# Graph-attention head 1 gets its own vector buffer, head 2's weights come in two halves: a transfer schedule is rearranged

## The chip, the core and the metric

The kernel is one program on one core of a Trainium2 chip. Its engines are named as in the profile: PE is TensorE (PEld its weight load), DVE VectorE, ACT ScalarE, POOL GpSimd, and SP the sync engine, whose queue issues nearly all large transfers. The metric is the device time of one execution in microseconds. Three executions of the kernel before took 346.65, 346.98 and 348.58 us; the median is 346.98.

## The reference

Four layers follow each other, each with a graph part and a feed-forward part, over 128 nodes with 768 features. The change touches only the first graph layer, a graph attention network (GAT) with eight heads. It comes after a layernorm of x:

```
def gat_layer(x, W, a_s, a_d, b, edge_index, concat):
    h = (x @ W).reshape(n, H, C)
    alpha_s = jnp.einsum('nhc,hc->nh', h, a_s)
    alpha_d = jnp.einsum('nhc,hc->nh', h, a_d)
    e = leaky_relu(alpha_s[src] + alpha_d[dst], 0.2)
    ... softmax over the edges of each dst, then
    msg = h[src] * alpha[:, :, None]
    out = segment_sum(msg, dst)
```

For head h there are 768 x 768 weights of the first product (2304 KB), two attention vectors of 768 (one for sources, one for targets) and 768 x 768 weights of the second layer's product, into which the eight heads are summed. All values are float32. Heads are counted from 0 here, so the "second head" is head 1 and the "third head" is head 2.

## The kernel before, in words

Everything is written out by hand: each engine has its own list of instructions, and semaphores order them against each other. x sits transposed in `xT` as six chunks. The first product of a head, x times its weights, is `head_product` (the matmuls of L1591; for head 0 they stand at L1654). It runs over six chunks of the contraction, first for one part of the output columns (512, six matmuls) and then for the rest (256, six more); a float32 matmul shows as two instructions in the trace. ACT copies the result into `h1`, whose halves alternate by head (`par`), and signals `h_rows`. DVE's `head_alphas` (L855, L857) multiplies those rows with the head's two attention vectors in `avec` and sums. These two numbers per node are turned by PE in `score_row` (L1599), DVE and ACT make the masked softmax (`head_softmax`, L867 to L877), PE turns it (`turn_attention`, L1605), aggregates (`aggregate_head`, L1613), DVE adds the bias (L885, signal `z_ready`) and applies the activation in three steps, and PE runs the second product (`head_second`, L1625).

The heads are pipelined: while PE multiplies head h+1, the attention of head h is computed beside it. PE's instructions are strictly in order. During head 1's first product PE also counts the edges (`count_edges`, 33 small bf16 matmuls at L1661) after three chunks and takes head 0's `score_row` after four; during head 2's first product head 1's `score_row` stands behind three chunks. That `score_row` waits for `alpha_ready` (head 1's numbers), for `score_sum`, and for `z_ready` of head 0, which on DVE stands behind head 1's `head_alphas`.

The transfers go through SP's queue in program order. Weights land in ring slots: the first products alternate between slots 0 and 1, the second products between 2 and 3. `x` comes first, then head 0's weights in six pieces, the first half of head 1's weights (semaphore `w1_second_in`), the vectors of head 0, and the second half of head 1's weights (semaphore `w1_in1`). After that a loop over steps issues, for each step, the next head's first weights (behind `hprod`, the end of the product that used the slot), this head's vectors (behind `alpha_ready`, because there is one buffer `avec`) and the previous head's second weights. A semaphore rises by 16 with each transfer that has landed completely.

Of the kernel before, what the change touches and what calls it, by code (L numbers as in the profile page):

```python
# [18 lines left out]
ALU = mybir.AluOpType  # L19
# [3 lines left out]
P = 128  # L23
D = 768
C = D // P
UNIT = C * D
# [86 lines left out]
def build(nc, a, out):  # L113

    ctx = ExitStack()
    with ctx:
        def sb(name, shape, dt=F32):
            return ctx.enter_context(nc.sbuf_tensor(name, shape, dt))
# [12 lines left out]
        g3 = sb("g3", [P, D])  # L131
        g4 = sb("g4", [P, D])
        h1 = sb("h1", [P, 2 * D])
        h2 = sb("h2", [P, 2 * D])
        avec = sb("avec", [P, 2 * D])
        row0 = sb("row0", [P, D])
        row1 = sb("row1", [P, D])
        rows = sb("rows", [P, NROWS])
        cols = sb("cols", [P, NCOLS])
        shiftm = sb("shiftm", [P, 3 * P])  # L140
# [52 lines left out]
        def slot_part(k, lo=0, hi=UNIT, parts=P):  # L193

            return ring[0:parts, SLOT_AT[k] + lo:SLOT_AT[k] + hi]
# [20 lines left out]
        S = {}  # L216

        def s(name):

            if name not in S:  # L220
                S[name] = sem(name)
            return S[name]
# [95 lines left out]
        def wait(eng, name, value):  # L318

            if value >= 1:  # L320
                eng.wait_ge(s(name), value)
# [3 lines left out]
        def chained(eng, name, ins):  # L325

            used[name] += 1
            ins.then_inc(S[name], 1)
            eng.wait_ge(S[name], used[name])

        def first_chunk(c):

            return f"w1_first{c}_in" if c < C - 1 else "w1_in0"
# [9 lines left out]
        @block.sync  # L343
        def _(sp):
            def load_avec(h):

                wait(sp, "alpha_ready", h)
                sp.dma_start(avec[:], a["gat_a"][bass.ds(h, 1), :].broadcast_to([P, 2 * D])).then_inc(S["avec_in"], 16)

            def load_w1(h, par):  # L350

                if h >= 2:
                    sp.wait_ge(S["hprod"], h - 1)
                sp.dma_start(slot_part(par), a["gat_w1"][bass.ds(h, 1)].rearrange("o p n -> (o p) n")) \
                    .then_inc(S[f"w1_in{par}"], 16)

            def load_w2(h, par):

                if h >= 2:
                    sp.wait_ge(S["w2_used"], h - 1)  # L360
                sp.dma_start(slot_part(2 + par), a["gat_w2"][bass.ds(h, 1)].rearrange("o p n -> (o p) n")) \
                    .then_inc(S[f"w2_in{par}"], 16)

            def load_step(h, par):
                load_w1(h + 1, 1 - par)
                load_avec(h)
                load_w2(h - 1, 1 - par)

            def load_unit(u):
                slot = landed[u][0]  # L370
                for name, c0, parts, n in UNITS[u]:
                    to, of = slot_part(slot, c0, c0 + n, parts), a[name]
                    if name in SHARED:
                        lo, hi = SHARED[name]
                        to = to.rearrange("p (c n) -> p c n", c=C)[:, :, lo:hi]
                        of = of.rearrange("p (c n) -> p c n", c=C)
                    sp.dma_start(to, of).then_inc(S[f"slot{slot}_in"], 16)

            sp.dma_start(x[:], a["x"]).then_inc(S["x_in"], 16)

            w1_0 = a["gat_w1"][0:1].rearrange("o p n -> (o p) n")
            for c in range(C):
                sp.dma_start(slot_part(0, c * D, (c + 1) * D), w1_0[:, c * D:(c + 1) * D]).then_inc(S[first_chunk(c)], 16)
            half = UNIT // 2
            w1_1 = a["gat_w1"][1:2].rearrange("o p n -> (o p) n")
            sp.dma_start(slot_part(1, 0, half), w1_1[:, 0:half]).then_inc(S["w1_second_in"], 16)
            load_avec(0)
            sp.dma_start(slot_part(1, half, UNIT), w1_1[:, half:UNIT]).then_inc(S["w1_in1"], 16)
            for h in range(1, 7):
                load_step(h, h % 2)  # L390
            load_avec(7)
            load_w2(6, 0)
            sp.wait_ge(S["hprod"], 7)
            load_unit(0)
            load_w2(7, 1)
            load_avec(8)

            for u in (U_L1, U_L1W1A, U_L1W1B, U_L2, U_L1W2A, U_L1W2B, *range(U_L3A, len(UNITS))):  # L400
                if u == U_L1:
                    sp.wait_ge(S["hprod"], 8)
                if u == U_L1W1A:
                    sp.wait_ge(S["w2_used"], 7)
                if u == U_L1W1B:
                    sp.wait_ge(S["hprod"], 9)
                if u == U_L2:
                    sp.wait_ge(s("edges_summed"), 1)
                if u >= SLOTS:
                    sp.wait_ge(s(released[u - SLOTS][0]), released[u - SLOTS][1])  # L410
                if u - SLOTS == U_L2:
                    sp.wait_ge(s("w_quantised"), 1)
                load_unit(u)
            for n, (lo, hi) in enumerate(HALVES):
                sp.wait_ge(s("result_ready"), n + 1)
                sp.dma_start(out[:, lo:hi], xb[:, lo:hi]).then_inc(S["out_done"], 16)
            sp.wait_ge(S["out_done"], 32)
# [360 lines left out]
        def _(dve):  # L778
            def link(ins):
                chained(dve, "dve_step", ins)  # L780
# [68 lines left out]
            def head_alphas(h, par):  # L849

                wait(dve, "h_rows", h + 1)
                dve.wait_ge(S["avec_in"], 16 * h + 16)
                wait(dve, "alpha_ready", h)
                hp = h1[:, par * D:(par + 1) * D]
                link(nc.vector.tensor_tensor_reduce(g3[:], hp, avec[:, 0:D], 1.0, 0.0, ALU.mult, ALU.add,  # L855
                                                    alpha[:, par, 0:1]))
                nc.vector.tensor_tensor_reduce(g4[:], hp, avec[:, D:2 * D], 1.0, 0.0, ALU.mult, ALU.add,  # L857
                                               alpha[:, par, 1:2]).then_inc(S["alpha_ready"], 1)

            def head_softmax(h, par):  # L860
# [109 lines left out]

            share = cell("alpha_share", 4)
            dve.wait_ge(s("gat2_rows"), 1)
            dve.wait_ge(S["avec_in"], 16 * 9)
            dve.wait_ge(S["alpha_ready"], 8)
            for k in range(2):
                link(nc.vector.tensor_tensor_reduce(g3[:, 0:WIN], h1[:, 0:WIN], avec[:, k * D:k * D + WIN], 1.0, 0.0, ALU.mult,
# [509 lines left out]
        def _(pe):  # L1486
# [78 lines left out]
            def head_product(n, par, in_value, after_first=None, halfway=None):  # L1565

                if n == 1:
                    pe.wait_ge(S["w1_second_in"], 16)
                else:
                    pe.wait_ge(S[f"w1_in{par}"], in_value)  # L1570
                if n >= 2:
                    pe.wait_ge(S["h_rows"], n - 1)
                w = slot_part(par).rearrange("p (c n) -> p c n", c=C)
                at = 0 if par == 0 else WIN + 256
                parts = ((0, WIN), (WIN, D)) if par == 0 else ((256, D), (0, 256))
                for lo, hi in parts:
                    if lo != parts[0][0]:

                        if after_first is not None:
                            after_first()  # L1580
                        wait(pe, "h_rows", n)
                    for c in range(C):
                        if c == 3 and lo == parts[0][0] and halfway is not None:
                            halfway()
                        if n == 1 and c == 3 and lo == parts[0][0]:
                            pe.wait_ge(S["w1_in1"], in_value)
                        if n == 1 and c == 4 and lo == parts[0][0]:
                            score_row(0, 0)
                        if n == 1 and c == 3 and lo == parts[1][0]:
                            turn_attention(0)  # L1590
                        last = mm(ps[:, at + lo:at + hi], xT[:, c, :], w[:, c, lo:hi], start=(c == 0), stop=(c == C - 1))  # L1591
                return last

            def score_row(h, par):

                wait(pe, "alpha_ready", h + 1)
                wait(pe, "score_sum", h)
                wait(pe, "z_ready", h)
                tr(bank(7, P, 256), alpha[:, par, 0:1].broadcast_to([P, P]), ident) \  # L1599
                    .then_inc(s("score_row_ps"), 1)  # L1600

            def turn_attention(h):
                wait(pe, "attn_ready", h + 1)
                wait(pe, "attnT_ready", h)
                tr(bank(7, P, 384), att[:, 1, :], ident).then_inc(S["attnT_ps"], 1)  # L1605
# [527 lines left out]
            for n in range(2):  # L2133
                for c in range(C):
# [5 lines left out]
                    lo, hi = ((0, MLP + EVEN), (MLP + EVEN, MLP + D))[n]  # L2140
# [91 lines left out]
```

## Time and profile before

| what | value |
|---|---|
| three executions | 346.65, 346.98, 348.58 us |
| the profiled execution, its own time | 349.45 us |
| its span, first to last instruction | 347.4 us |
| PE busy | 336.5 us, 97% of the span |
| DVE busy | 174.6 us, 50% |
| ACT busy | 69.9 us, 20% |
| SP's queue q1 | 85.02 MB, 62.3% of 16 DMA engines over the span |
| mean granted clock of PE | 0.995 |

The span is 2.05 us shorter than the profiled execution's own time: that is what lies around the first and the last instruction. PE is nearly always busy, so an edit is worth something only where it moves PE's own instructions, or the clock at which they run. The rows give a start and a duration; an idle time stands in brackets with what ended it. Matmuls overlap by a little, so the distance between two starts, not the duration of a row, is what a group costs.

### The profile page before, as it was taken

Reading aid. Unit: us, or ns where it says so; the run is one execution under the profiler, and the core shown is the slowest. Engines: PE = TensorE matmul, PEld = TensorE weight load, DVE = VectorE, ACT = ScalarE, POOL = GpSimd, SP = SyncE. Lnnn points to the kernel's source line nnn. Section 1 sums busy time; section 2 is a strip of 40 time slices with the busy share of each in tenths; the row PEclk is TensorE's granted clock in tenths of the full one; section 3 lists DMA queues with packets and bytes.
Section 4 is the critical chain, followed back from the end, with each engine's and each line's share of the span. In section 5 each row is a group of like instructions: output and inputs, shape, how many; then the busy total and the mean of one; then the engine's idle time right before and its main releaser. Section 6 shows DMA issues by size and latency. Waiting matters only on the chain.

```text
span 347.4 us, 4190 instructions
## 1 busy us (share of the span) xinstructions
PE 336.5 (97%) x1588; PEld 213.9 (62%) x1588; DVE 174.6 (50%) x533; ACT 69.9 (20%) x164; POOL 39.7 (11%) x64
## 2 busy tenths in 40 slices
PE   7997999999999999999989999999999999999997
PEld 3573657575757576566656556576646598966654
DVE  3946253838474746655772483542852501163451
ACT  2011111020202020013120232014314412074020
POOL 4900000020000000223022000021240100000000
PEclk9998999999999999999999999999999999999999
DMA  8999999989884585999999977576717700000001
GB/s 283 428 359 434 430 416 422 417 338 352 303 339 189 210 352 194 422 374 367 366 431 420 361 273 270 171 272 247 272 32 267 286 32 2 0 0 3 0 0 45
DMA packets 12565, 90.18 MB, mean 260 GB/s; under 512 B 2953, under 2 KB 3478, under 8 KB 8578
## 3 DMA queue, kind: packets, MB, share of 16 engines
q1 hardware_dynamic: 10446, 85.02, 62.3%
q0 software_dynamic: 848, 3.61, 3.0%
q10 hardware_dynamic: 1252, 1.29, 1.1%
q8 instruction: 12, 0.20, 0.2%
q14 instruction: 7, 0.06, 0.0%
HBM read 89.53 MB, written 0.39 MB: 259 GB/s over the span
## 4 chain that ended last, share of the span: by engine, by line
PE 86%; DVE 9%; DMA 3%; issue 1%; POOL 1%; ACT 0%; DVEq 0%; POOLq 0%
PE ps L1625 16%; PE ps L1591 13%; PE ps L1561 7%; PE ps L2013 7%; PE ps L1799 5%; PE ps L1818 5%; DMA avec<-in_gat_a 3%; PE ps L1613 3%; DVE ring L847 3%; PE ps L2141 2%; PE ps L1690 2%; PE ps L2125 2%; PE ps L2084 2%; PE ps L1493 2%; PE ps L1932 2%; PE ps L1632 2%
## 5 line engine op out<-in xcount | busy, mean ns | idle before, releaser
L1591 PE MATMUL ps<-ring,xT 128*128 128x512 f32 (+1 forms) x168 | 58.3, 497 | 0.0
L1625 PE MATMUL ps<-ring,h 128*128 128x512 f32 (+1 forms) x168 | 55.6, 486 | 0.0
L1625 PEld LDWEIGHTS ps<-ring,h 128*128 128x128 f32 x168 | 31.2, 190 | 21.9 <-issue 20.1
L1591 PEld LDWEIGHTS ps<-ring,xT 128*128 128x128 f32 x168 | 31.4, 195 | 21.0 <-issue 18.8
L855 DVE CUSTOM_DVE_ANT_0 g<-h,avec 128x768 f32<-128x768 f32 x8 | 7.7, 958 | 37.9 <-ACT h L547 26.5
L547 ACT ACTIVATE h<-ps 128x768 f32<-128x768 f32 (+6 forms) x24 | 13.8, 577 | 54.7 <-PE ps L1591 14.9
L1561 PE MATMUL ps<-ring,xT 128*128 128x512 f32 (+1 forms) x72 | 24.1, 488 | 0.1
L947 DVE TENSOR_SCALAR ring<-ring,idxb,ewb 128x128 bf16<-128x128 bf16 x99 | 22.5, 312 | 0.0
L1561 PEld LDWEIGHTS ps<-ring,xT 128*128 128x128 f32 x72 | 13.4, 190 | 9.3 <-issue 8.4
L430 POOL TENSOR_TENSOR rstd<-var,mhalf 128x1 f32<-128x1 f32 x8 | 4.8, 599 | 113.5 <-DVE var L1443 53.4
L2013 PE MATMUL ps<-g,ring 128*128 128x128 f32 x144 | 16.4, 275 | 0.0
L1799 PE MATMUL ps<-ring,xT 128*128 128x384 f32 (+1 forms) x48 | 16.2, 495 | 0.1
L1818 PE MATMUL ps<-ring,h 128*128 128x512 f32 (+1 forms) x48 | 16.3, 490 | 0.0
L2013 PEld LDWEIGHTS ps<-g,ring 128*128 128x128 f32 x144 | 16.2, 192 | 0.0
L588 ACT ACTIVATE g<-g 128x768 f32<-128x768 f32 x8 | 6.7, 843 | 32.5 <-DVE g L889 32.5
L1799 PEld LDWEIGHTS ps<-ring,xT 128*128 128x128 f32 x48 | 9.0, 190 | 6.5 <-issue 2.3
L579 ACT ACTIVATE att<-att,soft 128x128 f32<-128x128 f32 x9 | 3.6, 402 | 46.1 <-DVE soft L872 46.1
L547 ACT ACTIVATE xT<-ps 128x256 f32<-128x256 f32 x18 | 6.9, 384 | 29.4 <-PE ps L1509 19.5
L1818 PEld LDWEIGHTS ps<-ring,h 128*128 128x128 f32 x48 | 8.8, 190 | 5.8 <-issue 5.3
L1613 PEld LDWEIGHTS ps<-attnT,h 128*128 128x128 f32 x96 | 12.0, 192 | 0.4
L1613 PE MATMUL ps<-attnT,h 128*128 128x128 f32 x96 | 12.0, 275 | 0.0
L1380 DVE TENSOR_TENSOR g<-ps,cols 128x768 f32<-128x768 f32 x2 | 1.9, 958 | 19.4 <-PE ps L2013 19.4
(419 smaller groups left out, 482.8 us busy)
## 6 DMA issues: line engine op xcount, KB each, us to landing
ring<-in_gat_w SPq DMA_DIRECT2D x14, 2304.0 KB, 11.0
avec<-in_gat_a SPq DMA_DIRECT2D x9, 768.0 KB, 9.9
ring<-in_l_w SPq DMA_DIRECT2D x3, 2304.0 KB, 21.3
ring<-in_gat_w SPq DMA_DIRECT2D x6, 384.0 KB, 6.2
ring<-in_gat_w SPq DMA_DIRECT2D x2, 1152.0 KB, 11.5
ring<-in_l_w SPq DMA_DIRECT2D x2, 1152.0 KB, 12.9
ring<-in_l1f_w1a SPq DMA_DIRECT2D x1, 2304.0 KB, 12.8
ring<-in_l1f_w1b SPq DMA_DIRECT2D x1, 2304.0 KB, 10.2
```

The lines of the kernel that those rows point to most:

```text
L547: return nc.scalar.activation(dst, src, ACT.Copy)
L847: nc.vector.tensor_tensor(dst, iota_rows, idxb[:, n, :].unsqueeze(2).broadcast_to([P, EC, P]), ALU.is_equal).then_inc(s("onehots"), 1)
L855: link(nc.vector.tensor_tensor_reduce(g3[:], hp, avec[:, 0:D], 1.0, 0.0, ALU.mult, ALU.add, alpha[:, par, 0:1]))
L947: last_ = nc.vector.tensor_scalar(oh_src[:, 1 + k, e, :], iotab, idxb[:, 1, e:e + 1], ewb[:, k, e:e + 1], ALU.is_equal, ALU.mult)
L1493: mm(bank(spare), some[:, 0:P], some[:, 0:WIN], start=True, stop=True)
L1561: last = mm(ps[:, at + lo:at + hi], xT[:, c, :], w[:, c, lo:hi], start=(c == 0), stop=(c == C - 1))
L1591: last = mm(ps[:, at + lo:at + hi], xT[:, c, :], w[:, c, lo:hi], start=(c == 0), stop=(c == C - 1))
L1613: last = mm(ps[:, 6 * WIN + c * P:6 * WIN + (c + 1) * P], h1[:, par * D + c * P:par * D + (c + 1) * P], attnT[:, par, :], start=True, stop ...
L1625: last = mm(ps[:, 4 * WIN + lo:4 * WIN + hi], h2[:, par * D + c * P:par * D + (c + 1) * P], w[:, c, lo:hi], start=(n == 0 and c == 0), sto ...
L1799: last_ = mm(bank(g, hi - lo), xT[:, c, :], weights[:, c, lo:hi], start=(c == 0), stop=(c == C - 1))
L1818: last_ = mm(ps[:, lo:hi], h2[:, g * H0 + c * P:g * H0 + (c + 1) * P], weights[:, 3 * (g % 2) + c, lo:hi], start=False, stop=(g == 3 and c ...
L2013: last_ = mm(to, weights[:, c, o * P:(o + 1) * P], operand(c), start=(c == 0), stop=(c == chunks - 1))
```

## The change

Head 1's two vectors get a buffer of their own, `row_pair`, which is the memory of `row0` and `row1` joined; its transfer is issued directly behind the second half of head 1's weights, with `x_in` as its semaphore. DVE's `head_alphas(1)` reads `row_pair` and waits for `x_in` at 32. As `avec` is no longer needed for head 1, head 2's vectors wait only for `alpha_ready` at 1. Head 2's first weights are issued as two halves, the first with the semaphore `w1_first0_in`. `head_product` has the waits for these.

```
@@ -133,8 +133,8 @@
-        row0 = sb("row0", [P, D])
-        row1 = sb("row1", [P, D])
+        row_pair = sb("row_pair", [P, 2 * D])
+        row0, row1 = row_pair[:, 0:D], row_pair[:, D:2 * D]
@@ -344,7 +344,7 @@
-                wait(sp, "alpha_ready", h)
+                wait(sp, "alpha_ready", h if h > 2 else h - 1)
@@ -386,7 +386,14 @@
             sp.dma_start(slot_part(1, half, UNIT), w1_1[:, half:UNIT]).then_inc(S["w1_in1"], 16)
-            for h in range(1, 7):
+            sp.wait_ge(S["x_in"], 16)
+            sp.dma_start(row_pair[:], a["gat_a"][1:2, :].broadcast_to([P, 2 * D])).then_inc(S["x_in"], 16)
+            w1_2 = a["gat_w1"][2:3].rearrange("o p n -> (o p) n")
+            sp.wait_ge(S["hprod"], 1)
+            sp.dma_start(slot_part(0, 0, half), w1_2[:, 0:half]).then_inc(S["w1_first0_in"], 16)
+            sp.dma_start(slot_part(0, half, UNIT), w1_2[:, half:UNIT]).then_inc(S["w1_in0"], 16)
+            load_w2(0, 0)
+            for h in range(2, 7):
                 load_step(h, h % 2)
@@ -849,12 +856,16 @@
-                dve.wait_ge(S["avec_in"], 16 * h + 16)
+                if h == 1:
+                    dve.wait_ge(S["x_in"], 32)
+                else:
+                    dve.wait_ge(S["avec_in"], 16 * max(h, 1))
                 wait(dve, "alpha_ready", h)
+                vectors = row_pair if h == 1 else avec
@@ -970,7 +981,7 @@
-            dve.wait_ge(S["avec_in"], 16 * 9)
+            dve.wait_ge(S["avec_in"], 16 * 8)
@@ -1566,6 +1577,8 @@
                 if n == 1:
                     pe.wait_ge(S["w1_second_in"], 16)
+                if n == 2:
+                    pe.wait_ge(S["w1_first0_in"], 32)
                 else:
                     pe.wait_ge(S[f"w1_in{par}"], in_value)
@@ -1582,8 +1595,8 @@
-                        if n == 1 and c == 3 and lo == parts[0][0]:
-                            pe.wait_ge(S["w1_in1"], in_value)
+                        if n in (1, 2) and c == 3 and lo == parts[0][0]:
+                            pe.wait_ge(S[f"w1_in{par}"], in_value)
```

PE's list at the end of head 0's product and the start of head 1's, before (`ps<-ring,xT` are first products, `ps<-ring` the edge count, `ps<-shiftm,alpha` a score row):

```order
L1654 MATMUL ps<-ring,xT 128x256
L1591 MATMUL ps<-ring,xT 128x512 [waits w1_second_in]
L1591 MATMUL ps<-ring,xT 128x512 x2
L1661 MATMUL ps<-ring 128x128 [waits onehots]
L1661 MATMUL ps<-ring 128x128 x32
L1591 MATMUL ps<-ring,xT 128x512 [waits w1_in1]
L1599 MATMUL ps<-shiftm,alpha 128x128 [waits alpha_ready]
```

and with the change:

```order
L1667 MATMUL ps<-ring,xT 128x256
L1604 MATMUL ps<-ring,xT 128x512 [waits w1_in1,w1_second_in]
L1604 MATMUL ps<-ring,xT 128x512 x2
L1674 MATMUL ps<-ring 128x128 [waits onehots]
L1674 MATMUL ps<-ring 128x128 x32
L1604 MATMUL ps<-ring,xT 128x512 [waits w1_in1]
L1612 MATMUL ps<-shiftm,alpha 128x128 [waits alpha_ready]
```

The instructions are the same, in the same order. What differs is a wait: the first matmul of head 1's product names `w1_in1` beside `w1_second_in`, since the `else` now belongs to the test for head 2.

PE's list at the start of head 2's product, before:

```order
L1591 MATMUL ps<-ring,xT 128x512 [waits h_rows,w1_in0]
L1591 MATMUL ps<-ring,xT 128x512 x2
L1599 MATMUL ps<-shiftm,alpha 128x128 [waits z_ready,score_sum,alpha_ready]
L1591 MATMUL ps<-ring,xT 128x512 x3
L1605 MATMUL ps<-shiftm,att 128x128 [waits attnT_ready,attn_ready]
```

and with the change:

```order
L1604 MATMUL ps<-ring,xT 128x512 [waits h_rows,w1_first0_in]
L1604 MATMUL ps<-ring,xT 128x512 x2
L1612 MATMUL ps<-shiftm,alpha 128x128 [waits z_ready,score_sum,alpha_ready]
L1604 MATMUL ps<-ring,xT 128x512 [waits w1_in0]
L1604 MATMUL ps<-ring,xT 128x512 x2
L1618 MATMUL ps<-shiftm,att 128x128 [waits attnT_ready,attn_ready]
```

Here the wait for `w1_in0` has moved from the first matmul to the fourth, behind the score row, and `w1_first0_in` stands at the first.

SP's queue from the first half of head 1's weights on, before:

```order
L386 DMA ring<-in_gat_w 128x2304
L348 DMA avec<-in_gat_a 128x1536
L388 DMA ring<-in_gat_w 128x2304
L354 DMA ring<-in_gat_w 128x4608 [waits hprod]
L348 DMA avec<-in_gat_a 128x1536 [waits alpha_ready]
L361 DMA ring<-in_gat_w 128x4608
L354 DMA ring<-in_gat_w 128x4608 [waits hprod]
L348 DMA avec<-in_gat_a 128x1536 [waits alpha_ready]
L361 DMA ring<-in_gat_w 128x4608
```

and with the change:

```order
L386 DMA ring<-in_gat_w 128x2304
L348 DMA avec<-in_gat_a 128x1536
L388 DMA ring<-in_gat_w 128x2304
L390 DMA row_pair<-in_gat_a 128x1536 [waits x_in]
L393 DMA ring<-in_gat_w 128x2304 [waits hprod]
L394 DMA ring<-in_gat_w 128x2304
L361 DMA ring<-in_gat_w 128x4608
L354 DMA ring<-in_gat_w 128x4608 [waits hprod]
L348 DMA avec<-in_gat_a 128x1536 [waits alpha_ready]
L361 DMA ring<-in_gat_w 128x4608
```

Head 1's vectors have moved ahead of head 2's weights and wait only for `x_in`; head 0's second weights follow head 2's weights directly; and head 2's vectors stand directly behind head 3's weights.

## Rows read from the trace of the kernel before

**Rows 1.** Waits, 0 to 60 us: who waits, for whom; total us, times, longest.
```profile
PE ps L1599 <- DVE g L885: 2.1, 1, 2.1
```

**Rows 2.** Timeline of PE, 7 to 48 us: start, duration, engine, line, operation, [idle before].
```profile
7.77 7.91 PE L1654 MATMUL ps<-ring,xT 128*128 128x512 f32 x24
15.52 2.74 PE L1591 MATMUL ps<-ring,xT 128*128 128x512 f32 x6
18.09 2.01 PE L1661 MATMUL ps<-ring 128*128 128x128 bf16 x33
19.93 1.08 PE L1591 MATMUL ps<-ring,xT 128*128 128x512 f32 x2
...
26.74 2.84 PE L1591 MATMUL ps<-ring,xT 128*128 128x512 f32 x6
31.68 0.45 PE L1599 MATMUL ps<-shiftm,alpha 128*128 128x128 f32 x1 [2.10 <-DVE g L885]
31.92 4.30 PE L1591 MATMUL ps<-ring,xT 128*128 128x512 f32 x6
36.06 0.27 PE L1605 MATMUL ps<-shiftm,att 128*128 128x128 f32 x1
...
47.84 0.27 PE L1599 MATMUL ps<-shiftm,alpha 128*128 128x128 f32 x1
```

**Rows 3.** Timeline of SP's queue: issue start, duration.
```profile
5.21 0.53 SPq L388 DMA_DIRECT2D ring<-in_gat_w  x1
15.71 0.33 SPq L354 DMA_DIRECT2D ring<-in_gat_w  x1
19.11 0.33 SPq L348 DMA_DIRECT2D avec<-in_gat_a  x1
...
30.69 0.33 SPq L348 DMA_DIRECT2D avec<-in_gat_a  x1
```

**Rows 4.** DMA issues at 5.21, 15.71, 19.11, 30.69: KB, us from issue to landing.
```profile
ring<-in_gat_w SPq DMA_DIRECT2D x1, 1152.0 KB, 13.2
...
ring<-in_gat_w SPq DMA_DIRECT2D x1, 2304.0 KB, 11.0
...
avec<-in_gat_a SPq DMA_DIRECT2D x1, 768.0 KB, 9.5
...
avec<-in_gat_a SPq DMA_DIRECT2D x1, 768.0 KB, 10.7
```

**Rows 5.** Timeline of DVE, 28 to 42 us.
```profile
28.70 0.96 DVE L855 CUSTOM_DVE_ANT_0 g<-h,avec 128x768 f32<-128x768 f32 x1 [5.15 <-DMA avec<-in_gat_a]
...
30.58 0.95 DVE L885 TENSOR_TENSOR g<-ps,cols 128x768 f32<-128x768 f32 x1
...
32.17 0.35 DVE L867 SCALAR_TENSOR_TENSOR att<-ps,alpha,absent 128x128 f32<-128x128 f32 x1
...
34.16 0.28 DVE L877 TENSOR_SCALAR att<-att,soft 128x128 f32<-128x128 f32 x1
...
41.55 0.96 DVE L855 CUSTOM_DVE_ANT_0 g<-h,avec 128x768 f32<-128x768 f32 x1 [6.23 <-issue]
```

**Rows 6.** Timeline of ACT: head 1's rows are copied.
```profile
25.58 0.81 ACT L547 ACTIVATE h<-ps 128x768 f32<-128x768 f32 x1 [1.02 <-PE ps L1591]
```

**Rows 7.** Windows: busy of PE, PEld, DVE, ACT, POOL; PEclk, DMA share, GB/s.
```profile
17.00:18.00 1.00, 1.00 (x3) 0.29 (x2) 0.97 (x2) 0.00 (x0) 0.94 (x2) 1.00 0.50 138
31.00:32.00 1.00, 0.32 (x2) 0.35 (x3) 0.96 (x2) 0.00 (x0) 0.00 (x0) 0.82 0.90 387
...
34.00:35.00 1.00, 1.00 (x2) 0.34 (x1) 0.96 (x3) 0.00 (x0) 0.00 (x0) 0.50 0.86 369
35.00:36.00 1.00, 1.00 (x3) 0.33 (x2) 0.32 (x1) 0.00 (x0) 0.00 (x0) 0.97 1.20 516
181.00:184.00 3.00, 2.57 (x15) 2.02 (x16) 1.05 (x3) 0.96 (x3) 2.53 (x4) 1.00 0.99 417
```

**Rows 8.** Timeline of PE around a later, shorter idle.
```profile
181.43 1.57 PE L1518 MATMUL ps<-absent,xn 128*128 128x128 f32 x12 [1.10 <-DVE absent L1192]
```

More of the change, by code:

```diff
@@ L851, in head_alphas @@
                 wait(dve, "h_rows", h + 1)
-                dve.wait_ge(S["avec_in"], 16 * h + 16)
+                if h == 1:
+                    dve.wait_ge(S["x_in"], 32)
+                else:
+                    dve.wait_ge(S["avec_in"], 16 * max(h, 1))
                 wait(dve, "alpha_ready", h)
+                vectors = row_pair if h == 1 else avec
                 hp = h1[:, par * D:(par + 1) * D]
-                link(nc.vector.tensor_tensor_reduce(g3[:], hp, avec[:, 0:D], 1.0, 0.0, ALU.mult, ALU.add,
+                link(nc.vector.tensor_tensor_reduce(g3[:], hp, vectors[:, 0:D], 1.0, 0.0, ALU.mult, ALU.add,
                                                     alpha[:, par, 0:1]))
-                nc.vector.tensor_tensor_reduce(g4[:], hp, avec[:, D:2 * D], 1.0, 0.0, ALU.mult, ALU.add,
+                nc.vector.tensor_tensor_reduce(g4[:], hp, vectors[:, D:2 * D], 1.0, 0.0, ALU.mult, ALU.add,
                                                alpha[:, par, 1:2]).then_inc(S["alpha_ready"], 1)
```

## The prediction

> **What bounds the kernel now.** The table of busy shares comes first: PE is busy for 97% of the span, so only time that PE waits, or time at a lower clock, can be won. The view of waits then names the one large wait of the first 60 us: PE's score row of head 1 (L1599) waits 2.1 us for DVE's L885 [rows 1]. The timelines follow it back. On PE, three chunks of head 2's product start at 26.74, the score row at 31.68 [rows 2]. On DVE, L855 of head 1 starts at 28.70, after 5.15 us idle that a transfer into avec ended; L885, behind it, is done at 30.58 + 0.95 = 31.53 [rows 5]. The rows that L855 multiplies were ready at 25.58 + 0.81 = 26.39 [rows 6]. The vectors were issued at 19.11 and landed 9.5 later, at 28.6 [rows 3, 4]. So the late vectors of head 1 set PE's stall. The windows show its second price: the granted clock is 0.82 in the slice in which PE resumes, 0.50 through 34 to 35, and 0.97 in the next [rows 7], which is TensorE's lower level, 1.2 instead of 2.4 GHz. From the score row of head 2 on (47.84 [rows 2]) PE runs through the heads without a listed wait.
>
> **What the change removes.** Six matmul instructions of three chunks take 18.09 - 15.52 = 2.57 us start to start at full clock [rows 2]. Without the stall the score row would start at 26.74 + 2.57 = 29.31, not 31.68: 2.37 us. From the score row to the turning of the attention (L1605) it is 36.06 - 31.68 = 4.38 us. At full clock it would be 0.12 (half of the 0.24 between 31.68 and 31.92) + 2.57 = 2.69, so the low clock cost 1.69 us. Together 4.06 us can go.
>
> **What it adds, and this decides.** PE's order with its waits shows that head 1's product now waits for both halves of its weights before its first matmul; before, the second half was asked for only after three chunks and the edge count. That half was issued at 5.21 and took 13.2, so it landed at 18.4 [rows 3, 4]. Before, PE began head 1's product at 15.52 and asked for the second half at 19.93 [rows 2], 1.5 us after the landing: no wait. Now it stands. DVE resumed 0.1 us after its vectors landed (28.70 against 28.6), so PE resumes at 18.5: 3.0 us late. Behind that matmul stand the edge count, on which DVE's mask waits, the score row of head 0 and all later work of PE; nothing can slip past. New transfers don't delay the landing: head 1's vectors are issued behind this half.
>
> The bounds of this wait: between 17 and 18 us the DMA engines were only half busy, at 138 GB/s [rows 7], so most of the bytes were in by about 17.4, and the wait would be 2.0 us if all engines were as early. At the other end 4.0, with the straggler as late again. I take 3.0, which is the row itself. The Trainium skill (DMA: Bandwidth & Descriptors, the section on why a DMA increments its semaphore by 16) says that a transfer is only in when every one of the engines that share it has written. By that rule the end is the last engine's, 18.4 and 3.0 us; by the mean rate it would be about 2.0. The trace agrees with the rule: the share falls at 17 us and the landing is at 18.4.
>
> Then the clock. The trace has a stall of 2.10 us listed, followed by the low clock, and one of 1.10 us at 181.43 [rows 8] around which the window reads 1.00 [rows 7]. The new wait is longer than both, so I take the drop as happening, at the price of the nearest row, 1.7 us. Bounds: 0 as after the 1.10 us idle; and, if the three chunks and the edge count all run at half clock, their whole time again, 2.57 + (19.93 - 18.09) = 4.4 us.
>
> So everything behind the edge count is 3.0 + 1.7 = 4.7 us late.
>
> **What is left of the old stall.** With 4.7 us, head 1's rows are ready at 31.09, and L855 starts at about 31.15, its vectors being long there (issued at about 5.8, ahead of head 2's weights). L885 is done 31.53 - 28.70 = 2.83 us later, at 33.98, and PE, which took 0.15 us to follow it before, starts the score row at 34.13. PE itself would be there at 26.74 + 4.7 + 2.57 = 34.01: a remainder of 0.1. The softmax's last step ends 34.16 + 0.28 - 28.70 = 5.74 us behind L855 [rows 5], at 36.89, where PE, at full clock, wants it at 34.13 + 2.69 = 36.82; with the hand-over some 0.3 us more. Remainder 0.4 in all; bounds 0 and 1.
>
> **The rest, at nothing.** Head 2's weights landed at 15.71 + 11.0 = 26.7 [rows 3, 4], exactly as PE came to them at 26.74. With 768 KB of vectors ahead of them they land up to 2 us later (768 KB at the 417 GB/s of a full window is 1.9 [rows 7]), at 28.6, less the thin stretch at 17 to 18 that they fill. But PE comes at 31.4, and to the second half at 34.1; the halves hide nothing that the delay doesn't hide already. Without the delay the first half would be the cover: 1152 KB at the same rate are in 2.8 us before the rest. Head 2's vectors were issued at 30.69, landed 10.7 later and DVE took them at 41.55 [rows 3 to 5]. They are now issued behind head 3's weights, whose issue slips with the product of head 1, by 4.7, to about 30.5; so they land as before, 41.4. PE wants that score row at 47.84 + 1. The wait for `x_in` before the new issue costs nothing: PE multiplies x from 7.77 on [rows 2], and SP has nothing else to issue before 15.71. The two halves are one more issue in SP's queue, about 0.4 us, which nothing waits for.
>
> **The sum.** 3.0 + 1.7 - 4.06 + 0.4 = +1.0 us. On the profiled execution, 349.45 becomes about 350.5 and the span 347.4 about 348.4. Against the median of the executions shown, which is 2.5 us below the profiled one, I add the same difference: 346.98 + 1.0 = 348.0. That is 0.3%. About 0.5%, 1.7 us, is what a measurement of this kernel can tell from no change.
>
> **The rivals.**
> 1. *Slower.* The low clock that the change removes is one execution's. In the timed ones, 2.5 us shorter than the profiled, the 2.1 us stall may leave the clock at full, so that only 2.37 + 0 is won, while the longer new wait at 15.5 still pulls it down: 3.0 + 1.7 - 2.37 + 0.4 = +2.7, 349.7. It decides as soon as the two clock terms together cost 0.7 us more than in the sum, where they cancel; here they cost 1.7 more. The same happens if the low level lasts through the edge count too (+3.7, 350.7). For it: the new wait is longer than the old. Against it: the one trace shows the drop at the old stall.
> 2. *Clock kept, full wait.* 3.0 - 4.06 + 0.4 = -0.7, 346.3, no change that can be told. Against it: a shorter idle lost the clock.
> 3. *Faster.* The second half lands early, at 17.4, and the clock stays: 2.0 - 4.06 + 0.4 = -1.7, 345.3. For it: the half-busy window at 17 to 18.
> 4. *The change does only what its words say*: head 1's second half is in by 15.5 and the new wait is empty. Then -4.06 + 0.4, less up to half a us because head 2's vectors are late next: 343.5. Against it: a landing at 18.4, 2.9 us off.
>
> The Trainium skill (TensorE: Matmul & The Clock Gate, part 1) states that the clock is reconsidered at moments that run free of the kernel's own start, so that the same kernel meets a different number of slow matmuls from run to run. By that rule either clock term may be missing in an execution, and the sum moves between -0.7 and +2.7; by the rows of the one trace it is +1.0. No run here shows it yet; rivals 1 and 2 carry it by rows.
>
> **How the numbers follow.** Forecast (the clock terms cancel to within 0.7 us): 56%. Rival 1: 30%. Rival 2: 7%. Rival 3: 4%. Rival 4: 3%. So slower by over 0.5% is 0.31 with the forecast's upper edge, faster 0.07, within 0.62. The range runs from 345.9, between rivals 3 and 2, to 349.9, just over rival 1; the forecast's own range is 347.3 to 348.7.
>
> **What would show it.** Right: PE idle for about 3 us before the first matmul of head 1's product, ended by the transfer of head 1's weights at about 18.4; a granted clock of 0.5 from there for some 3 us; no listed wait of more than 0.3 us at head 1's score row, nor DVE waiting for vectors at head 1; every start from 60 us on about 1 us later than before. Wrong: head 1's product begins at 15.5; or the clock reads 1.00 behind the new wait (346.3); or the later heads start more than 2 us late, which points to rival 1 or to a transfer that I hold to be in time.

## The result and the profile after

| kernel | median of 7 executions | lowest to highest |
|---|---|---|
| before | 346.65 us | 345.68 to 348.58 |
| changed | 349.93 us | 348.59 to 352.06 |

The change makes the kernel slower: the ratio is 1.0089, with a 95% interval from 1.0066 to 1.0111. The forecast of 348.0 us was 1.9 us short; the first rival, 349.7, is where the time came out, on the upper edge of the range that was given (345.9 to 349.9). The profiled execution took 350.16 us with a span of 348.3, against 349.45 and 347.4.

In the waits of the changed kernel (0 to 60 us), the row that stood for PE is gone, and a new one has taken its place. DVE waits with it, for the edge count:

```profile
PE ps L1604 <- DMA ring<-in_gat_w: 3.2, 1, 3.2
DVE count L937 <- PE ps L1674: 6.2, 1, 6.2
```

PE's timeline, with the bracket giving idle time and its releaser:

```profile
7.37 8.01 PE L1667 MATMUL ps<-ring,xT 128*128 128x512 f32 x24
18.56 4.38 PE L1604 MATMUL ps<-ring,xT 128*128 128x512 f32 x6 [3.18 <-DMA ring<-in_gat_w]
22.73 2.17 PE L1674 MATMUL ps<-ring 128*128 128x128 bf16 x33
24.74 1.08 PE L1604 MATMUL ps<-ring,xT 128*128 128x512 f32 x2
...
31.52 2.74 PE L1604 MATMUL ps<-ring,xT 128*128 128x512 f32 x6
34.21 0.29 PE L1612 MATMUL ps<-shiftm,alpha 128*128 128x128 f32 x1
34.35 2.74 PE L1604 MATMUL ps<-ring,xT 128*128 128x512 f32 x6
36.92 0.31 PE L1618 MATMUL ps<-shiftm,att 128*128 128x128 f32 x1
...
48.75 0.27 PE L1612 MATMUL ps<-shiftm,alpha 128*128 128x128 f32 x1
```

Against [rows 2]: head 1's product starts at 18.56 instead of 15.52. Its three chunks take 22.73 - 18.56 = 4.17 us instead of 2.57. The edge count begins at 22.73 (18.09 before), the next matmuls at 24.74 (19.93). So everything is 4.8 us late there; the prediction had 4.7. Then most of it comes back: head 1's score row follows its three chunks without a listed wait (34.21, 2.69 us after their start), and the next three chunks take 2.57 us again, so that the turning stands at 36.92 against 36.06. From there the shift stays: head 2's score row at 48.75 against 47.84, 0.9 us.

The transfer that ends the wait, as SP's queue issues it, and its landing (KB, us from issue to landing):

```profile
5.11 0.45 SPq L388 DMA_DIRECT2D ring<-in_gat_w  x1
5.60 0.63 SPq L390 DMA_DIRECT2D row_pair<-in_gat_a  x1
```

```profile
ring<-in_gat_w SPq DMA_DIRECT2D x1, 1152.0 KB, 13.3
```

5.11 + 13.3 = 18.4, exactly as before (5.21 + 13.2, [rows 3, 4]). The transfer has not become slower; PE has begun to need it sooner. The granted clock (the last three columns of the windows are PEclk, DMA share, GB/s) falls behind the new wait, and is full where the old stall was:

```profile
19.00:20.00 1.00, 1.00 (x3) 0.38 (x2) 0.00 (x0) 0.00 (x0) 0.00 (x0) 0.83 1.10 455
20.00:21.00 1.00, 1.00 (x2) 0.33 (x1) 0.00 (x0) 0.00 (x0) 0.00 (x0) 0.50 0.97 406
...
22.00:23.00 1.00, 1.00 (x5) 0.29 (x4) 0.00 (x0) 0.00 (x0) 0.00 (x0) 0.50 1.03 433
31.00:35.00 4.00, 4.00 (x16) 2.02 (x15) 3.67 (x8) 0.50 (x2) 0.00 (x0) 1.00 0.96 323
```

And on DVE, head 1's vectors are no longer waited for; its three steps follow the copy of the rows by ACT, which ended at 31.19:

```profile
31.23 0.96 DVE L866 CUSTOM_DVE_ANT_0 g<-h,row_pair 128x768 f32<-128x768 f32 x1 [2.88 <-ACT h L554]
...
33.11 0.95 DVE L896 TENSOR_TENSOR g<-ps,cols 128x768 f32<-128x768 f32 x1
...
36.57 0.28 DVE L888 TENSOR_SCALAR att<-att,soft 128x128 f32<-128x128 f32 x1
```

So in the profiled execution the three large steps of the sum are there, and its total: spans 348.3 - 347.4 = 0.9 us against 1.0 forecast. What the sum does not give is the measured difference of the medians, 3.3 us. The profiled execution of the kernel before (349.45) lay above all seven timed ones.

### The profile page after: what moved, and what is told of

Read it like the earlier page. It is cut to its first block, busy times and chain, and to the rows that moved or that the text cites. A ratio compares the mean times of both kernels' runs of the same rounds, so it can differ in the third digit from the quotient of the medians.

```text
span 348.3 us, 4192 instructions
## 1 busy us (share of the span) xinstructions
PE 336.2 (97%) x1588; PEld 212.9 (61%) x1588; DVE 174.6 (50%) x533; ACT 69.9 (20%) x164; POOL 40.3 (12%) x64
## 4 chain that ended last, share of the span: by engine, by line
PE 88%; DVE 5%; DMA 4%; SPq 1%; issue 1%; POOL 0%; ACT 0%; DVEq 0%
PE ps L1604 16%; PE ps L1638 16%; PE ps L1572 7%; PE ps L2026 7%; PE ps L1812 5%; PE ps L1831 5%; DMA ring<-in_gat_w 4%; PE ps L1626 3%; PE ps L2154 2%; PE ps L1703 2%; PE ps L2138 2%; PE ps L2097 2%; PE ps L1945 2%; PE ps L1645 2%; PE ps L2059 1%; PE ps L1728 1%
## 5 line engine op out<-in xcount | busy, mean ns | idle before, releaser
L866 DVE CUSTOM_DVE_ANT_0 g<-h,avec 128x768 f32<-128x768 f32 x7 | 6.7, 958 | 30.2 <-ACT h L554 30.2
```

## Experiments

Every run has 12 executions, the profiled one among them, and each ratio is to executions of the kernel before on the same chip in the same series. Where two edited kernels are compared, it is by their medians, some of them from different series; the kernel before had 346.65, 346.86, 346.98 and 346.78 us in the four series. Beside the time, each execution gives its span and the mean granted clock; in the traces, a mean of 0.995 is one stretch at the low level (0.50) in the whole span.

### The kernel before, again

No edit.

> The kernel before, unchanged, to see what its timed executions look like beside the one whose trace the prediction used. Theory A (the trace read was an unusual execution: its stall of 2.1 us at head 1's score row drew the low clock, most others do not): most executions show a mean granted clock of 1.0 and about 346.3 us, those with 0.995 or less show 348 us or more, and a profile with clock 1.0 has a span near 344.5 us with an idle at the score row of head 1 clearly under 2.1 us. Theory B (the execution read was typical, the 2.4 us lie later in the program): clocks of 0.995 throughout, a stall of 2.1 us again.

Measured: 347.24 us (345.80 to 349.09, 12 executions), ratio 0.9994 [0.9974, 1.0015]. The profiled execution, 349.09, again has the stall and the low clock:

```profile
26.47 2.74 PE L1591 MATMUL ps<-ring,xT 128*128 128x512 f32 x6
31.32 0.29 PE L1599 MATMUL ps<-shiftm,alpha 128*128 128x128 f32 x1 [2.11 <-DVE g L885]
31.45 4.44 PE L1591 MATMUL ps<-ring,xT 128*128 128x512 f32 x6
35.72 0.27 PE L1605 MATMUL ps<-shiftm,att 128*128 128x128 f32 x1
```

35.72 - 31.32 = 4.40 us from score row to turning, as the 4.38 of [rows 2]. But it is the only one of the 12 with a clock of 0.995. Of the 35 other executions of this kernel in the series one has it (span 347.4); of 35 in the second series, none. The spans of the first 35 at full clock go from 343.9 to 346.5, and the median of all 35 is 344.8. So the execution whose trace was read is not like most others: the other 11 of this run have no low clock, and spans of 343.8 to 345.7, 1.4 to 3.3 us shorter. That is Theory A's first half, though the time is 0.9 us above the 346.3 it gave. Both profiled executions of this kernel have the low clock and nearly none of the others, which is hardly chance; what sets them apart isn't known. This run has no trace at full clock; the fills below give two.

### The change without its added wait

```
@@ the changed kernel, head_product
-                if n == 2:
+                elif n == 2:
                     pe.wait_ge(S["w1_first0_in"], 32)
```

> The changed kernel with one wait taken back: the first matmul of head 1's product waits for the first half of its weights alone, as before. Prediction's reasoning: the 3.2 us stall at 15.4 us and its clock loss go, and so does the old stall at head 1's score row; PE is then 3.7 us earlier at head 2's product than in the changed kernel and reaches a stall of about 0.6 us at the turning of head 2 (its vectors land at about 41). Theory A: 344.5 to 345.5 us, that is 1 to 2 us below the kernel before and 4.5 to 5.5 below the changed one. Theory B: 343 to 344 us. Rival (the new order of transfers costs by itself): no faster than 346.5.

Measured: 345.96 us (345.68 to 346.43), ratio 0.9966 [0.9949, 0.9984], all clocks 1.0, spans 343.7 to 344.3. One keyword is worth 4.0 us against the changed kernel's median. PE in its profiled execution:

```profile
7.71 7.91 PE L1667 MATMUL ps<-ring,xT 128*128 128x512 f32 x24
15.45 2.74 PE L1604 MATMUL ps<-ring,xT 128*128 128x512 f32 x6
...
26.65 2.74 PE L1604 MATMUL ps<-ring,xT 128*128 128x512 f32 x6
29.34 0.29 PE L1612 MATMUL ps<-shiftm,alpha 128*128 128x128 f32 x1
...
32.05 0.32 PE L1618 MATMUL ps<-shiftm,att 128*128 128x128 f32 x1
...
61.14 5.32 PE L1604 MATMUL ps<-ring,xT 128*128 128x512 f32 x12
66.61 0.33 PE L1618 MATMUL ps<-shiftm,att 128*128 128x128 f32 x1 [0.16 <-DVE att L888]
```

Head 1's product starts at 15.45, the score row of head 1 at 29.34 without a wait. The spans lie within 0.6 us, where those of before spread over 2.6 at full clock: most of what varied there was the stall, as the traces further down show. The time is 0.5 us above Theory A's range, because I had set the range from the lowest executions and not from the median. The stall that I expected at the turning of head 2 isn't there; 0.3 us stand one head later (66.61 - 61.14 = 5.47 us against 5.15). Small losses like it, at head 3 or head 4, are in four traces of kernels that come there earlier, and not in the changed kernel's, where the same distance is 5.15 us. So the change, without its wait, loses about 0.3 us of its gain again.

### The kernel before with the added wait alone

```
@@ the kernel before, head_product
                 if n == 1:
                     pe.wait_ge(S["w1_second_in"], 16)
-                else:
-                    pe.wait_ge(S[f"w1_in{par}"], in_value)
+                pe.wait_ge(S[f"w1_in{par}"], in_value)
```

> The kernel before with the one wait added: head 1's product waits for both halves of its weights before its first matmul; nothing else differs. Theory A: the wait of about 3 us at 15.5 stands, and head 1's vectors, issued at 19.1 as before, are now in before their rows are ready, so the rest is as in the changed kernel: 349 to 350.5 us, equal to the changed kernel within 0.7. Rival (the wait is not what costs, the order of transfers does): within 1 us of the kernel before.

Measured: 350.06 us (348.21 to 350.55), ratio 1.0067 [1.0044, 1.0090]. PE:

```profile
18.38 4.51 PE L1590 MATMUL ps<-ring,xT 128*128 128x512 f32 x6 [2.88 <-DMA ring<-in_gat_w]
22.72 2.01 PE L1660 MATMUL ps<-ring 128*128 128x128 bf16 x33
...
31.35 2.74 PE L1590 MATMUL ps<-ring,xT 128*128 128x512 f32 x6
34.04 0.29 PE L1598 MATMUL ps<-shiftm,alpha 128*128 128x128 f32 x1
```

The same wait, the same low clock behind it (4.34 us for three chunks), and then no stall at head 1's score row, although its vectors are loaded as before: the delay hides them. With the order of the transfers untouched the kernel is as slow as the changed one, 349.93. So this wait alone explains the loss, and beside it the rest of the change is hidden.

This run also gives the clock's price apart from the wait's: five executions at full clock have spans of 346.3 to 347.0, seven at 0.995 have 347.9 to 348.6; the medians differ by 1.7 us. In the changed kernel it is three (346.6 to 346.8) and four (347.9 to 349.9). The last of these has a mean clock of 0.990 and is 3.2 us longer than at full clock, as two low stretches would make it; no trace shows it.

### The changed kernel with PE kept busy during the wait

```
                 if n == 1:
+                    stay_warm(12)
                     pe.wait_ge(S["w1_second_in"], 16)
```

> The changed kernel with 12 small bf16 matmuls of 128x512 (about 2.6 us) ahead of head 1's first wait, so that PE isn't idle while it waits for the weights; they write a bank that nobody reads. It keeps the wait and takes away the drop of the clock. Theory (the low clock behind the new wait costs 1.7 us where it occurs, and it occurs in about half of the executions): mean clock 1.0 in all executions, 348.4 to 348.9 us, 1 to 1.5 us below the changed kernel's median, with a smaller spread. Rival (the clock is of no account, only the wait): 349.9 as the changed kernel.

Measured: 349.07 us (348.39 to 350.94), ratio to before 1.0065 [1.0043, 1.0086]. PE:

```profile
15.15 2.75 PE L1504 MATMUL ps<-shiftm 128*128 128x512 bf16 x11
18.16 2.81 PE L1605 MATMUL ps<-ring,xT 128*128 128x512 f32 x6 [0.26 <-DMA ring<-in_gat_w]
20.81 2.01 PE L1675 MATMUL ps<-ring 128*128 128x128 bf16 x33
```

The three chunks take 2.65 us; the wait ends at 18.16, 0.4 us earlier than in the changed kernel's trace. All twelve clocks are 0.998 or more. The spans have a median of 346.8, that of the full-clock executions of the changed kernel (346.7), where its own median is 347.9. The median time is 0.9 us below the changed kernel's, and 0.2 us above the range expected, since in four of these executions 2.7 to 3.6 us lie outside the span, where it is about 2.0 elsewhere; why is not known. The wait and the clock are two separate costs, and the fill takes away the second only.

### How long the old stall is in the timed executions

```
@@ the kernel before, score_row
+                if h == 1:
+                    wait(pe, "score_sum", h)
+                    stay_warm(5, 3)        # second kernel: stay_warm(10, 3)
                 wait(pe, "alpha_ready", h + 1)
```

> The kernel before, with 5 bf16 matmuls of 128x512 (1.08 us at full clock) put into PE's idle time ahead of head 1's score row, written to a bank that nobody reads. They cost nothing as long as the idle time is at least as long. Theory C (in the timed executions that idle time is about 1.2 to 1.5 us, because head 1's vectors land about a microsecond earlier than in the profiled one): hidden, within 0.3 us of the kernel before. Theory D (the idle time is 2.1 us in them too and only the low clock is missing): hidden too, so the same; this run is the control for the next, and shows that the fill keeps the clock at 1.0 in the profiled one as well, whose span is then about 345.5 instead of 347.2.

> As the run before, with 10 such matmuls (2.16 us). Theory C: the fill is longer than the idle time by 0.7 to 1 us, and the median rises by that: 347.5 to 348. Theory D: still hidden, 346.9 as the kernel before (within 0.3).

Measured: with 5, 347.28 us (346.22 to 349.10), ratio 1.0015 [0.9997, 1.0034]; with 10, 347.41 us (347.13 to 347.97), ratio 1.0012 [0.9996, 1.0028], before 346.98. By the intervals alone, both theories stand: the rise with 10, 0.4 us, lies between them. With 5 the spans have a median of 345.0, against 345.1 before, so that fill costs nothing. The spread with 10, and the two traces, decide. With 10 all twelve spans lie between 345.2 and 345.9: the fill has become a floor, and PE goes on at 31.40 in the profiled execution:

```profile
26.67 2.74 PE L1591 MATMUL ps<-ring,xT 128*128 128x512 f32 x6
29.46 2.11 PE L1493 MATMUL ps<-shiftm 128*128 128x512 bf16 x9
31.40 0.27 PE L1602 MATMUL ps<-shiftm,alpha 128*128 128x128 f32 x1
```

If the idle time of the kernel before always reached to 31.4 or beyond, no execution of it could have a span under 345.2. 20 of 35 do in this series (343.9 to 345.1), and 20 of 35 in the first. So in more than half of the timed executions the stall is shorter than in the one that was read. Against 343.9 without the stall, the medians of 344.8 and 345.1 leave about 1.0 us of span for it.

The traces show the stall itself. With ten matmuls, DVE and the landing of head 1's vectors, which were issued at 19.00:

```profile
27.13 0.96 DVE L855 CUSTOM_DVE_ANT_0 g<-h,avec 128x768 f32<-128x768 f32 x1 [3.63 <-DMA avec<-in_gat_a]
...
29.02 0.95 DVE L885 TENSOR_TENSOR g<-ps,cols 128x768 f32<-128x768 f32 x1
```

```profile
avec<-in_gat_a SPq DMA_DIRECT2D x1, 768.0 KB, 8.0
```

The vectors landed at 27.0, not at 28.6, and L885 was done at 29.97. With the 0.15 us that PE took to follow it in [rows 2], the score row would have stood at 30.12 without the fill, where 26.67 + 2.69 = 29.36 is the time without a stall (2.69 as in the changed kernel with and without its wait): an estimate of 0.8 us, against 31.68 - 29.43 = 2.25 by the same count in the execution that was read. With five, the fill was shorter than the stall, and PE still waited:

```profile
31.13 0.29 PE L1602 MATMUL ps<-shiftm,alpha 128*128 128x128 f32 x1 [0.62 <-DVE g L885]
```

That is 1.8 us behind 29.37, at a full clock; 0.7 us more went at head 3, so the span was 346.0 and not the 345.5 expected. Theory C holds in its reason: the vectors land earlier than in the execution that was read, and by how much varies.

### The change without the halves

```
@@ the run without the added wait, SP's queue
-            sp.dma_start(slot_part(0, 0, half), w1_2[:, 0:half]).then_inc(S["w1_first0_in"], 16)
-            sp.dma_start(slot_part(0, half, UNIT), w1_2[:, half:UNIT]).then_inc(S["w1_in0"], 16)
+            sp.dma_start(slot_part(0), w1_2).then_inc(S["w1_in0"], 16)
```

and the waits of `head_product` as before.

> The changed kernel with head 1's wait as before and without the halves of head 2's weights: only the vector buffer and the order of the transfers are left of the change. Reasoning: in the changed kernel's trace head 2's second half was in at 25.9, before PE reaches that product at 26.7, so the halves hide nothing: 345.96 as with the halves (within 0.3). Rival (the whole of the weights lands after 26.7 and PE waits for it): 0.5 to 1.5 us more, 346.5 to 347.5.

Measured: 346.06 us (345.59 to 346.48), ratio 0.9970 [0.9960, 0.9981]. The halves are worth nothing measurable (346.06 against 345.96); the whole gain is the vectors'. In its trace the undivided weights were in at 15.52 + 10.8 = 26.3, just ahead of PE, which took them at 26.52.

### The added wait made shorter

```
@@ the changed kernel, SP's queue
-            load_avec(0)
             sp.dma_start(slot_part(1, half, UNIT), w1_1[:, half:UNIT]).then_inc(S["w1_in1"], 16)
+            load_avec(0)
```

> The changed kernel, its added wait included, with one exchange in SP's queue: the second half of head 1's weights goes ahead of head 0's vectors (768 KB). The half lands some 1.9 us earlier, at about 16.5, so the new wait is about 1.2 us instead of 3.2 and too short for the low clock. DVE takes head 0's vectors, now landing last, about 1.5 us later, but what waits for them stands behind the edge count. Theory (the wait and its clock are the whole of the cost): 347.0 to 347.8 us, clock 1.0. Rival (another part of the change costs): 349 or more.

Measured: 346.77 us (346.49 to 347.42), ratio 0.9996 [0.9982, 1.0010], all clocks 1.0. PE:

```profile
7.37 8.01 PE L1667 MATMUL ps<-ring,xT 128*128 128x512 f32 x24
16.56 2.81 PE L1604 MATMUL ps<-ring,xT 128*128 128x512 f32 x6 [1.18 <-DMA ring<-in_gat_w]
19.21 2.01 PE L1674 MATMUL ps<-ring 128*128 128x128 bf16 x33
```

The half lands 2.0 us earlier (PE at 16.56 instead of 18.56), 1.2 us of idle do not draw the low clock, and 3.2 us of the loss are gone. The time is 0.2 us under the range expected. What remains against the run without the wait, 0.8 us, fits this shorter wait (16.56 - 15.45 = 1.1 us) less the 0.3 us that the other loses at head 3.

### The buffer without the new place in the queue

```
@@ the run without the halves, SP's queue
-            sp.wait_ge(S["x_in"], 16)
-            sp.dma_start(row_pair[:], ...).then_inc(S["x_in"], 16)
             ...
             sp.dma_start(slot_part(0), w1_2).then_inc(S["w1_in0"], 16)
+            sp.wait_ge(S["x_in"], 16)
+            sp.dma_start(row_pair[:], ...).then_inc(S["x_in"], 16)
```

> The kernel of the run 'vectors only' (head 1's wait as before, no halves), with the transfer of head 1's vectors put back behind head 2's weights in SP's queue. It still has its own buffer and so waits for nothing but x: it is issued at about 16, not at 19.1. Theory P (place in the queue decides: in the trace of before the queue was full, and the vectors followed head 2's weights by 1.9 us, which is their own length): they land about where they did, within 1 us of 28.5, and the time is 346.6 to 347.2 us, as the kernel before. Rival W (the wait for the buffer decides): they land 3 us earlier and the time is 346.0 us, as with the new place.

Measured: 347.36 us (346.49 to 349.13), ratio 1.0014 [0.9996, 1.0033]. SP's issues and the landing of head 1's vectors:

```profile
15.73 0.33 SPq L391 DMA_DIRECT2D ring<-in_gat_w  x1
16.10 0.43 SPq L393 DMA_DIRECT2D row_pair<-in_gat_a  x1
```

```profile
ring<-in_gat_w SPq DMA_DIRECT2D x1, 2304.0 KB, 9.7
row_pair<-in_gat_a SPq DMA_DIRECT2D x1, 768.0 KB, 11.3
```

They are issued 3.0 us earlier than in [rows 3] and land at 27.4: 1.2 us earlier than in the execution that was read, but no earlier than with the ten matmuls above (27.0), where they were issued at 19.00. In both traces, and in [rows 4], they land 1.9 or 2.0 us behind head 2's weights (25.4 here, 25.1 and 26.7 there). The median is no better than before's 346.78; it is 0.2 us above Theory P's range, and the landing is 1.1 us from its 28.5, but Rival W's 346.0 is ruled out. A buffer of one's own takes away a wait of SP's queue, but the transfer still lands behind head 2's weights. In the run without the halves the vectors, ahead of them, were issued at 5.68 and were in at 19.9. The place in the queue is what helps. PE in this profiled execution:

```profile
26.73 2.74 PE L1601 MATMUL ps<-ring,xT 128*128 128x512 f32 x6
30.52 0.30 PE L1609 MATMUL ps<-shiftm,alpha 128*128 128x128 f32 x1 [1.05 <-DVE g L895]
30.65 2.74 PE L1601 MATMUL ps<-ring,xT 128*128 128x512 f32 x6
```

It has a shorter stall than the execution that was read, 1.05 us, at a full clock, and a span of 344.9. That is one trace of what the medians of before (344.8, 345.1) are like, though of another kernel.

## Why the prediction was right in sign and short in size

- *The added wait, 3.0 us*: right. 3.04 in the profiled execution (18.56 against 15.52), ended by the transfer named, which landed when it was said to. At full clock the changed kernel's timed executions pay 2.8 (346.7 against 343.9 without the wait), a little less, as the small loss at head 3 goes with it.
- *The low clock behind it, 1.7 us*: right in size, 1.7 between the executions with and without it, and the mean clock shows it in 11 of 19 executions (changed kernel and the wait alone). The sum took it as certain.
- *What the change removes, 4.06 us*: this is the step that failed. "2.37 us" and "the low clock cost 1.69 us" were read from one execution. Both were there when the kernel was profiled again, but of the 98 other executions whose clock is known (11, 35, 35 and 17) one shows the low clock. In these the removed part is about 1.0 us: 344.8 to 345.1 of span against 343.9. The mechanism was right (late vectors, a stall at head 1's score row), the term four times too large.
- *The remainder, 0.4 us*: too large, within its bounds of 0 and 1. The 0.1 us at the score row is there (2.69 us behind its product's start, not 2.57), as in every traced kernel without the stall. The 0.3 us at the turning is not: 36.92 - 34.21 = 2.71 us, where 2.69 was worked out for PE unhindered. That the total was 0.9 and not 0.8 us is due to the delay, 4.8 us instead of 4.7.
- *The rest at nothing*: right. The halves give 0.1 us, within the noise; the vectors of head 2 were in time. Not foreseen was the 0.3 us at head 3, which shows only without the wait.
- *Scaling by the median*: the prediction noted that the profiled execution lay 2.5 us above the median, and added the same difference to both. By their size, the 2.5 us were the very clock (1.7) and the excess of the stall that it credited to the change. Rival 1 said this of the clock, at 30%; it gave +2.7, and +3.3 was measured. It had left the old stall at 2.37 and only its clock at nothing; the stall was shorter too. That 349.93 lies at the range's edge is rival 1's doing: the range had been drawn to just over it. The forecast itself, in which the two clock terms cancel, did not happen in the timed executions.

With the corrected terms: 2.8 + 1.7 - 1.0 = +3.5 for an execution with the low clock, +1.8 for one without; the median of seven fell among the first, four of them. Had one more of the seven kept the full clock, which 8 of 19 did, the median would have been near 348.8 and the forecast 0.8 us off: how far off it looks is in part luck.

What stays open is why head 1's vectors land later in the profiled executions of the kernel before. The semaphore's rises in the traces narrow it down. Fourteen of the vectors' sixteen rises are in at 26.9 in the execution that was read and at 26.7 in the second one; with five, with ten matmuls and in the last run it is at 26.3, 26.7 and 26.8. The last rise comes at 28.6, 28.2, 28.0, 27.0 and 27.4. So the bulk lands at nearly the same time in all five, and the last one or two of the sixteen shares make the difference. Head 2's weights, ahead of them, are late in the same order: complete at 26.7, 26.1, 25.9, 25.1 and 25.4. Why one share falls behind, and why it fell furthest in the two profiled executions of this kernel, was not tried.

## What to carry to other kernels

When a branch is added in a chain of conditions, compare the list of waits per instruction, not the count of instructions: here an `else` that changed its owner moved one wait ahead of three chunks and 33 small matmuls and cost 4.0 us, four times what the edit had to win. Where the profiled execution is slower than the timed ones by more than the edit is worth, the difference may be the very stall that the edit removes; take the clock and the span of several executions before crediting it. And in this full queue, giving a transfer its own buffer was worth nothing measurable until its place in the queue moved too.

## What the runs showed of the hardware

The low clock (1.2 GHz) followed an idle time of PE of 3.2 and of 2.9 us in the two traces that have one, and one of 2.1 us in both profiled executions that had it. None of the idles of 1.05, 1.1, 1.2 and 1.4 us drew it in the traces that have them. In the two kernels with the wait of about 3 us, the mean clock is low in 11 of 19 executions; the other eight have no trace, but their spans (346.3 to 347.0 us) carry the wait and not the clock. The same kernel on the same data thus has two times 1.7 us apart, by whether the clock falls. Twelve bf16 matmuls of 128x512 on a spare bank, 2.6 us of work with no result, put into the wait, kept the mean clock at 0.998 or more in 12 of 12.

A transfer of 768 KB behind one of 2304 KB had fourteen of its sixteen rises in 1.7, 1.5, 1.7, 0.3 and 0.6 us before the last, in five traces: one or two late shares held it up by that much.
